# First chunk of a gather-fed cross network: its first layer split into two halves of two tiles, one half beside the gathers of the fourth tile

## What is computed

```python
target  = item_table[item_id] + gelu(ln(item_emb @ mm_w + mm_b))
seq_emb = item_table[item_seq]                          # (B, 50, 128), gathered
x       = concatenate([t, seq_emb, t - seq_emb, t * seq_emb])
scores  = where(item_seq == 0, -1e9, relu(x @ aw1 + ab1) @ aw2 + ab2)
hist    = einsum('bs,bsd->bd', softmax(scores), seq_emb)
se      = sparse * w            # 5 features of 128, gated by a squeeze network
bil     = 10 products of pairs  # (se_i @ bil_W_i) * se_j
dnn_in  = concatenate([se, bil])                        # (B, 15 * 128)
xc = dnn_in
for i in range(2):                                      # the two cross layers
    xc = dnn_in * (xc @ cross_K[i] + cross_bias[i]) + xc   # cross_K[i]: 1920 x 1920
h = gelu(ln(xc @ w1 + b1)); h = gelu(ln(h @ w2 + b2)); out = sigmoid(h @ w3 + b3)
```

## Time and profile before

| | us |
|---|---|
| median of 3 runs | 2201.66 (2201.39 to 2207.11) |
| profiled execution, its own time | 2186.45 |
| its span | 2184.4 |
| PE busy | 1942.2 (89%) |
| DVE busy | 1330.2 (61%) |
| POOL busy | 904.3 (41%) |
| ACT busy | 899.4 (41%) |

### The profile page before, as it was taken

How to read it: one execution, slowest core, us unless ns; L and a number is a source line. 1 busy time by engine, 2 the same in 40 slices (tenths; PEclk the granted TensorE clock), 3 DMA queues, 4 the chain that set the end, 5 groups by cost and what they waited for, 6 DMA issues and landing times. The chain is left out here.

```text
span 2184.4 us, 32774 instructions
## 1 busy us (share of the span) xinstructions
PE 1942.2 (89%) x9609; PEld 1530.2 (70%) x9609; DVE 1330.2 (61%) x2211; ACT 899.4 (41%) x1954; POOL 904.3 (41%) x854
## 2 busy tenths in 40 slices
PE   2654553999999999999999999999999999999995
PEld 1433432777777787777777887777777888888884
DVE  3444444467677766666777766657777654445542
ACT  1333333354444434655444334654445243322222
POOL 6666666566655550455665520555551000000000
PEclk6656655999999999999999999999999999999997
DMA  4111111334343463234343462334333352333330
GB/s 154 45 45 44 42 45 41 101 112 115 111 121 102 134 213 94 80 101 120 103 123 119 123 201 76 98 89 128 118 103 94 115 169 79 92 98 98 99 85 1
DMA packets 99536, 220.31 MB, mean 101 GB/s; under 512 B 21648, under 2 KB 27040, under 8 KB 99232
## 3 DMA queue, kind: packets, MB, share of 16 engines
q1 hardware_dynamic: 62960, 136.89, 21.0%
q0 software_dynamic: 27136, 55.63, 10.1%
q10 hardware_dynamic: 9264, 25.69, 3.1%
HBM read 205.27 MB, written 12.85 MB: 100 GB/s over the span
## 5 line engine op out<-in xcount | busy, mean ns | idle before, releaser
L391 POOL DMA_INDIRECT e<-in_item_table,idx_all x800 | 852.9, 1066 | 689.5 <-issue 334.6
L1056 DVE TENSOR_TENSOR Wl<-raw,Wh 128x640 fp32r<-128x640 f32 (+1 forms) x420 | 338.1, 805 | 293.6 <-DVEq L1055 293.0
L766 ACT ACTIVATE Wh<-raw 128x640 fp32r<-128x640 f32 (+1 forms) x420 | 301.7, 722 | 497.9 <-ACTq L765 494.2
L516 PE MATMUL xps<-X0h,Wh 128*128 128x512 f32 x900 | 365.6, 406 | 6.7 <-PEq L514 6.7
L516 PE MATMUL xps<-X1h,Wh 128*128 128x512 f32 x900 | 359.6, 400 | 0.0
L518 PE MATMUL xps<-X0h,Wl 128*128 128x512 f32 x900 | 353.7, 393 | 0.0
L517 PE MATMUL xps<-X0l,Wh 128*128 128x512 f32 x900 | 352.9, 392 | 0.0
L518 PE MATMUL xps<-X1h,Wl 128*128 128x512 f32 x900 | 351.4, 390 | 0.0
L517 PE MATMUL xps<-X1l,Wh 128*128 128x512 f32 x900 | 351.1, 390 | 0.0
L729 ACT ACTIVATE e<-e,pw 128x128 f32<-128x128 f32 x800 | 242.6, 388 | 15.4 <-ACTq L122 15.4
L433 PE MATMUL aps<-ident,e 128*128 128x128 f32 x700 | 111.9, 295 | 106.8 <-issue 90.4
(11 more groups left out here) (145 smaller groups left out, 2227.0 us busy)
## 6 DMA issues: line engine op xcount, KB each, us to landing
raw<-in_cross_K SPq DMA_DIRECT2D x360, 320.0 KB, 2.9
raw<-in_w SPq DMA_DIRECT2D x60, 256.0 KB, 2.7
e<-in_item_table,idx_all POOLq DMA_INDIRECT x800
dnn_scratch<-dn ACTq DMA_DIRECT2D x12, 960.0 KB, 4.5
x1f<-dnn_scratch ACTq DMA_DIRECT2D x3, 2048.0 KB, 9.7
x1f<-dnn_scratch ACTq DMA_DIRECT2D x3, 1792.0 KB, 15.4
dn<-in_embT SPq DMA_DIRECT2D x1, 1024.0 KB, 5.3
img_scratch<-dn ACTq DMA_DIRECT2D x1, 1024.0 KB, 5.3
```

Of the source, the lines that this page charges most:

```text
L391: nc.gpsimd.indirect_dma_start(out=dst, out_offset=None, in_=table, in_offset=bass.IndirectOffsetOnAxis(ap=idx_all[:, t, s:s + 1], axis=0) ...
L516: m0 = mm(out, wh, Xh[:, 0:T, k, :], start=(k == 0), stop=False)
L766: af(Wh[:, split_slot(w), 0:n], raw[:, rs, 0:n], ACT.Copy).then_inc(hi_done, 1)
L1056: v.tensor_tensor(Wl[:, rs, 0:n], raw[:, rs, 0:n], Wh[:, slot, 0:n].bitcast(F32), ALU.subtract).then_inc(lo_done, 1)
```

## The change

The opening is cut to 18 steps and makes tiles 0 to 2 (`OPEN_TILES = 3`). Then 15 "early" steps follow: chunk 0's first layer for tiles 0 and 1 alone, 256 columns (`tiles = (0, EARLY)`). Beside them the groups of tile 3 are done, in early steps 1, 3, 5, 7, 9, and two groups of tile 4, in 11 and 13. Tile 2's tail falls into early steps 0 to 4 and tile 3's into 10 to 14; both use `tail_hi` and `tail_lo` there. Chunk 0's own steps 0 to 14 then do the first layer for tiles 2 and 3, again 256 columns, and 15 to 29 the second layer for all four, 512 columns as before. The other groups of tiles 4 to 7 stand in chunk 0's steps 1, 3, 5; 7, 8, 9, 11, 12; 14 to 18; 20 to 24. Chunks 1 to 3 are unchanged.

The weights of the first layer are streamed twice: 45 more units (`EXTRA`) for SP, ACT's `w_hi` and DVE's `w_lo`. Matmuls of the first layer in chunk 0 are 1350 of 256 columns where 675 of 512 stood. Tile 3's gathers now wait after every five, as those of later tiles.

The core of the diff:

```diff
-GROUP_STEPS = {
-    4: [[1 + 6 * j + g for g in range(NG)] for j in range(4)],
...
-}
+EARLY = 2
+EXTRA = FEATS * UNITS
+LEAD = 3
+OPEN_TILES = 3
+OPEN_STEPS = LEAD + NG * OPEN_TILES
+EARLY_AT = OPEN_STEPS
+CHUNK_AT = EARLY_AT + FEATS
+
+
+def group_steps():
+
+    where = [[LEAD + NG * j + g for g in range(NG)] for j in range(OPEN_TILES)]
+    where.append([EARLY_AT + k for k in (1, 3, 5, 7, 9)])
+    where.append([EARLY_AT + k for k in (11, 13)] + [CHUNK_AT + k for k in (1, 3, 5)])
+    where += [[CHUNK_AT + k for k in ks] for ks in ((7, 8, 9, 11, 12), (14, 15, 16, 17, 18), (20, 21, 22, 23, 24))]
+    for c in range(1, CHUNKS - 1):
+        where += [[CHUNK_AT + STEPS * c + 1 + 6 * j + g for g in range(NG)] for j in range(4)]
+    return where
...
 def make_plan():
...
+    plan = [Step(None, k) for k in range(OPEN_STEPS)]
+    plan[-1].last = True
+    for k in range(FEATS):
+        plan.append(Step(0, k, (0, EARLY), k * UNITS))
+        plan[-1].early = True
     for c in range(CHUNKS):
-        plan += [Step(c, k) for k in range(STEPS)]
...
+        for k in range(STEPS):
+            tiles = (EARLY if c == 0 and k < FEATS else 0, TILES[c])
+            plan.append(Step(c, k, tiles, EXTRA + c * STREAM + k * UNITS))
...
-                        if (s + 1) % (GRP if t < TILES[0] else SUB) == 0:
+                        if (s + 1) % (GRP if t < OPEN_TILES else SUB) == 0:
...
+                if p.pair is not None and p.pair < TILES[0]:
+                    tail_lo(p.pair)
+                    if p.pair == TILES[0] - 1:
+                        dve.sem_inc(x_ready, FEATS)
```

More of the change, by code:

```diff
@@ L606, in opening_step @@
                     tail_turn2(p.lift)
-                if p.grp:
+                if p.last:
+                    transposes(*p.grp, 0)
+                    transposes(*p.grp, 1)
+                    score()
+                elif p.grp:
                     transposes(*p.grp, 0)
@@ L616, in step @@
                 T, k = p.fc, p.k
-                products(p.chunk, p.layer, p.n, 0)
+                products(p, 0)
                 if T and 2 <= k < T + 2:
@@ L625, in step @@
                     transposes(*p.grp, 0)
-                products(p.chunk, p.layer, p.n, 1)
+                products(p, 1)
                 if p.grp:
@@ L637, in step @@
                     fc_w3(T)
-                products(p.chunk, p.layer, p.n, 2)
+                products(p, 2)
                 if T and 2 <= k < T + 2:
@@ L655, in _ @@
                 opening_step(p)
+            for p in early:
+                step(p)
             for c in range(CHUNKS):
@@ L842, in step @@
                     tail_copy(p.pair)
-                unit(c, 3 * k)
+                unit(p.first)
                 if p.fetch is not None:
@@ L855, in step @@
                     copy_eT(0)
-                unit(c, 3 * k + 1)
+                unit(p.first + 1)
                 if T and 2 <= k < T + 2:
@@ L1099, in unit, with unit_out @@
-            def unit(c, b):
-                if c * STREAM + b + LOOK < TOTAL:
-                    w_lo(c * STREAM + b + LOOK)
-            def unit_out(c, b):
-                if c * STREAM + b + LOOK < TOTAL:
+                low = v.tensor_tensor(some(Xl, p), fresh(p), some(Xh, p).bitcast(F32), ALU.subtract)
+                if not p.early:
+                    low.then_inc(x_ready, 1)
+            def unit(w):
+                if w + LOOK < TOTAL:
+                    w_lo(w + LOOK)
+            def unit_out(w):
+                if w + LOOK < TOTAL:
@@ L1181, in step @@
                 if prev:
[L1182 removed]
+                    x_sum(prev)
                 if p.summed:
```

173 lines of the change are left out of this document (88 added, 85 removed).

## The result

The changed kernel takes **2232.99 us**, median of four runs (2224.91 to 2238.63), beside 2204.39 (2201.39 to 2209.93) for the kernel before in the same session: ratio **1.0117, 95% interval 1.0093 to 1.0141**. Two later sessions gave 1.0093 (1.0069 to 1.0117) and 1.0096 (1.0079 to 1.0113). By these ratios it is slower by 20 to 26 us; the medians lie 28.6, 21.8 and 20.3 us apart. The forecast was 6.7 us more, 2208.4 us, with a range up to 2228; the time lies outside. The profiled execution of after has a span of 2222.7 us, against 2184.4 in the first trace of before.

What follows compares the result with a forecast made beforehand. It took chunk 0 as bound by PE and, within two or three us, by the gathers. Terms 13.9 + 3 - 1 - 10.2 + 1 = +6.7 us at w1's start gave 2208.4 us, range 2195 to 2228.

Steps and rivals of the forecast that it cites:

- The gathers: Tiles 3 to 7 pass POOL in 481.1 us instead of 467.2, +13.9 us; tile 8's first gather near 735.
- The 3 us for contention: Denser weight traffic slows the gathers of tiles 3 to 7: +3 us, between 0 and 10.9.
- The tail: From the last group's transposes to w1 of chunk 0, 75.5 us before: one bare step fewer, -10.2 us.
- The small step: A step of 256 columns takes PE 5.1 us, 8.5 at worst, with products 0.114 us apart.
- A bare group's chain: Early steps: one group's path from scores over DVE and hidden layer to scores again takes 18.9 us, level with gathers' 19.2.
- The store: Tile 7's feature store, one step later, delays the load behind it and ACT at w1's start: +1 us (0 to 3).
- POOL: The 45 added `w_lo` on DVE could stop POOL's gathers, up to 37 us; the trace pointed to far less.
- Chunks 1 to 3 only shift: Chunks 1 to 3 and the end stay unchanged and only move later, by the +6.7 us at w1's start.
- Why PE should keep up: Early steps and chunk 0: PE finishes each group before the next lands; two steps and a group 14.8 us, at worst 21.6.
- the second rival: Small steps fall behind, early steps to chunk 0's step 7, over about 22 us a group; 2236 us at 25; chance 0.10.
- PE and POOL run level: Kernel before, 430 to 719 us: chunk 0 is bound by PE and, within two or three us, by the gathers too.
- my sum's mechanism: Gathers set w1's start in chunk 0, +6.7 us; 2204 to 2219 us with its unknown costs; chance 0.81.

Runs made afterwards that it cites:

- before_third: The kernel before, unedited, run a third time as partner of the changed kernel in session 5: ratio 0.9996 to before, w1 of chunk 0 at 795.5 us.
- after_few: Changed kernel, of every five history-row gathers of tiles 3 to 15 only the first two issued, waits kept: ratio 1.0095 to before, w1 at 808.9 us.
- E13: Not a run: early step 13 of the changed kernel, where a group of tile 4 is transposed, at 412.3 us in its first trace.
- after_third: The changed kernel, unedited, run a third time, in session 5: ratio 1.0096 to before, w1 of chunk 0 at 809.1 us.
- after_no_low: Changed kernel without the weights' low part in the fifteen early steps (45 DVE subtractions and their product): ratio 1.0031 to before, w1 at 791.9 us.
- before_few: Kernel before, of every five history-row gathers of tiles 4 to 15 only the first two issued, waits kept: ratio 0.9999, w1 at 795.6 us.
- after_thin: Changed kernel without the product of the weights' high part with x's low part in the fifteen early steps: ratio 1.0091 to before, w1 at 810.3 us.
- before_lag: Kernel before, POOL in the opening's four tiles waiting after every five gathers for the five before them: ratio 1.0293, w1 at 854.9 us.

## Why the prediction was wrong, step by step

Right were these. **The gathers**: 481.1 + 3 - 1 us from 252 gave 735; tile 8 began at 736.90 and, undisturbed, at 732.39, 12.5 us later than in before_third, where the sum had 15.9. The 3 us for contention don't show. But that the gathers set w1's start, on which the sum rests, was wrong: after_few has tile 8 at 717.01 and w1 at 808.9 all the same. **The tail**: 65.3 us from the last group to w1, 66.2 and 65.3 measured. **The small step**: 5.1 us, 5.35 measured (products 0.12 us apart). **A bare group's chain**: 18.9 us, 18.8 measured. **The store**: +1 (0 to 3) at w1's start, +1.7 and +2.4 measured. **POOL**: I had weighed up to 37 us for the added `w_lo`; a gather took 1.09 us of POOL beside them (80.33 us for 74, after, E1 to E13), as the 1.10 before. So no such cost shows. The section of the Trainium skill that I had named for it (SBUF — State Buffer, "Who interferes with whom") goes on to infer that `tensor_tensor` does not hold up the making of DMA descriptors; I had left that out, and the trace agrees with it. **"Chunks 1 to 3 only shift"** held up to 3 to 6 us.

**The step that failed is "Why PE should keep up".** PE fell 43 us behind the gathers, and made up only 32 of them. The step allowed "lags from tails or the step before chunk 0, some 5 to 10 us", to be made up in steps 7 to 13. Late in the undisturbed trace of after_third was:

| group of | landed | transposes | late |
|---|---|---|---|
| E1 | 269.5 | 278.0 | 8.5 |
| E7 | 329.3 | 348.4 | 19.1 |
| E13 | 386.7 | 408.2 | 21.5 |
| C1 | 407.7 | 444.9 | 37.2 |
| C7 | 460.6 | 503.8 | 43.2 |
| C24 | 732.4 | 743.7 | 11.3 |

It starts 8.5 us late, because the opening's last groups are. Tile 2's tail and the heads share DVE and ACT with the first groups: 22.3, 23.5 and 24.6 us for three groups, where the chain was priced bare; that is 14 us over 18.8. From E13 to C1 there are three steps and not two: 36.7 us for a group, with tile 3's `tail_pairs` and `tail_lo` (1.68 and 2.16 us of DVE), behind which PE waits 4.59 us for `x_ready` before the first product of chunk 0 (two rows of DVE, one of PE):

```profile
428.41 1.68 DVE L1082 TENSOR_TENSOR dn<-dn,xps 128x512 f32<-128x512 f32 x4
...
432.75 2.16 DVE L1093 TENSOR_TENSOR X0l<-dn,X0h 128x1920 fp32r<-128x1920 f32 x1 [1.04 <-DVEq L1091]
...
435.30 0.55 PE L547 MATMUL xps<-X0h,Wh 128*128 128x256 f32 x1 [4.59 <-PEq L545]
```

That is 15.7 us more of lateness, and up to C7 6 more come. The tails, the heads and the third step stand in the plan and could have been summed; the lateness came to 43 us, not 5 to 10. That the tails and heads make the 14 us is read from the plan and the trace; no run leaves them out. In the second rival I had the place (early steps to C7), the point (28 us of lag) and a size (2236 at 25 us a group) and gave it 0.10, because I priced its causes at weight loads and the clock. Its sum doesn't close either: 58 us behind less the 20 that steps 7 to 24 were to give back leaves 38, not 28. They gave back 32 (43.2 late at C7, 11.3 at C24).

Weight loads were not the cause: with the clock at its upper level products start 0.12 us apart. The clock was a part. Behind waits of 4.06 and 6.58 us the granted clock was 0.50 (after_third, 285.9 to 290.4 and 334.3 to 338.1), the 1.2 GHz level, and products started 0.21 us apart. Over E1 to E13 that cost the products some 6 to 9 us (an estimate from the 0.09 us between the two spacings, and from all products that started later than 0.12 us), and the 25 products behind the wait of 4.59 us 2.3 more. How much of it lay in the path isn't shown. PE was busy 105.4 us in E1 to E13, 17.6 a group, where I had 14.8. (A group's own work in that sum is 2.3 + 1.0 + 1.1 = 4.4, not 4.5.)

Under it lies an error of reading. "Emptied" PE time in the opening was measured on PE, and the lists of DVE and ACT for a narrow step were summed for one chain and not with the tails and heads in the same queues. And "PE and POOL run level", read from the earlier trace rows, was a coincidence: without 60% of the gathers before takes 0.9999 of its time.

The rest follows. 732.4 + 65.3 = 797.7, w1's start by my sum's mechanism, and 11.3 late makes 809.1. Without the lag, and with the gathers as they were, the change would have been worth +2 us at w1, an estimate; with it, 14 there and 20 in all. The one run without lag at the end is after_no_low, with work left out. It is 25.5 us late at C7, but takes the last group as it lands (726.6). There w1 starts at 791.9, 3.8 us before before_few's, and its median is still 5 us above the kernel before (2196.65, 2191.63). So no run here shows a gain, even where PE keeps up at the end.

## What to carry to other kernels

Before work is moved beside other work, add up every in-order queue that serves both, with the tails that fall into the same steps, and the waits between the queues. Cutting a step's columns in half does not halve what is paid once per weight, and here it doubled the number of splits of the first layer. A count of busy time and short gaps does not show that a queue is the limit: hold it against a stretch in which it held nobody up, and take work out to see what comes of it. Four orders of the same work each took one wait away and brought another.

## What the runs showed of the hardware

- In some executions results of PE reach ACT and DVE late beside bursts of gathers. From the modelled end to the taker it is 0.20 us usually, up to 5.05 us beside bursts of five to ten gathers (after_thin), and 19 to 24 us in an opening in which POOL issued for 39 to 71 us without a pause (before_lag). There it is the change of PE's semaphores that comes late, four of them within 0.2 us (282.21 to 282.40); whether PE's work ended late too, or the signal alone, is open, and so is the cause. Hand-overs from ACT and DVE took 0.15 us at most in the same traces. Seen in traces of sessions 1 to 3, though not in the first of before, and in none of sessions 4 to 6, which had the same two kernels. The Trainium skill (SBUF — State Buffer, "Who interferes with whom") gives PE no port in common with any engine and names the shared port pair as the only contention; by it no such lateness would be expected, and the rows above show one.
- The kernel before took 2200.9 to 2204.4 us in sessions 1 to 3 and 2187.4 to 2191.6 in sessions 4 to 6, 9 to 17 us less. The ratio of the two kernels moved little: 1.0117 and 1.0093 in sessions 1 and 2, 1.0096 in session 5.
- fp32r products of 256 columns start 0.12 us apart at a granted clock of 1.00 (after_third, 353.2 to 356.0), about half of the 0.2275 of 512 columns, with their weight loads hidden, and 0.21 us apart at a granted clock of 0.50.
